# Probabilities turned as halves of 64 rows on two row groups, and new orders for four engines

## What is computed

```python
def dilated_mask(seq_len):           # SEGMENT_LENGTH = 64, DILATION_RATE = 4
    pos = jnp.arange(seq_len)
    seg = pos // SEGMENT_LENGTH
    local = seg[None, :] == seg[:, None]
    diff = jnp.abs(pos[None, :] - pos[:, None])
    dil = (diff > 0) & (diff % DILATION_RATE == 0) & (diff <= DILATION_RATE * SEGMENT_LENGTH)
    return jnp.where(local | dil, 0.0, -jnp.inf).astype(jnp.float32)
...
x = x + attention(_layernorm(x))     # 16 heads of 64, softmax over the allowed keys, then w_o
x = x + fp4_ffn(_layernorm(x))
x = x + gated_mixer(_layernorm(x))
x = x + token_mix(_layernorm(x))
```

## Time and profile before

| | us |
|---|---|
| median of 3 runs | 470.95 (470.03 to 474.9) |
| span of the profiled execution | 468.2 |
| TensorE busy | 443.3 |
| VectorE busy | 394.1 |
| ScalarE busy | 333.0 |
| GpSimd busy | 296.5 |

### The profile page before, as it was taken

How to read it: one execution, slowest core, us unless ns; L and a number is a source line. 1 busy time by engine, 2 the same in 40 slices (tenths; PEclk the granted TensorE clock), 3 DMA queues, 4 the chain that set the end, 5 groups by cost and what they waited for, 6 DMA issues and landing times.

```text
span 468.2 us, 17264 instructions
## 1 busy us (share of the span) xinstructions
PE 443.3 (95%) x6440; PEld 348.8 (74%) x6440; DVE 394.1 (84%) x1344; ACT 333.0 (71%) x975; POOL 296.5 (63%) x491
## 2 busy tenths in 40 slices
PE   7999699999999999999999899998987989999996
PEld 5687588888888888888787678887744757558775
DVE  5888598997988899799797697996899989998775
ACT  3678668778768777877786678695566579987533
POOL 4222576687576768667865587665669897674322
PEclk9999999999999999999999999999999999999999
DMA  6477952356345335445455564464000000000003
GB/s 224 175 254 201 276 122 53 75 115 123 75 84 110 74 74 109 81 78 109 86 116 122 110 135 90 77 123 91 1 1 0 0 2 0 2 0 2 1 0 91
DMA packets 136098, 40.53 MB, mean 87 GB/s; under 512 B 104976, under 2 KB 131024, under 8 KB 136016
## 3 DMA queue, kind: packets, MB, share of 16 engines
q1 hardware_dynamic: 135440, 38.38, 35.9%
q10 hardware_dynamic: 576, 1.05, 0.6%
HBM read 29.44 MB, written 9.96 MB: 84 GB/s over the span
## 4 chain that ended last, share of the span: by engine, by line
PE 59%; POOL 9%; DMA 8%; DVE 8%; ACT 7%; SPq 4%; issue 3%; ACTq 0%; POOLq 0%; DVEq 0%
PE psum L464 10%; PE psum L422 10%; PE psum L484 5%; PE psum L1186 5%; PE psum L498 5%; PE psum L495 4%; PE psum L510 4%; PE psum L403 4%; DMA st<-w_rows_dram 3%; DMA w_rows_dram<-st 3%; PE psum L1181 3%; ACT pband L569 3%; PE psum L405 2%; PE psum L404 2%; POOL area L1827 2%
## 5 line engine op out<-in xcount | busy, mean ns | idle before, releaser
L948 POOL TENSOR_SCALAR pband<-pband,fac 128x192 f32<-128x192 f32 x256 | 103.9, 424 | 84.8 <-DVE fac L771 84.7
L569 ACT ACTIVATE pband<-pband,st 128x192 f32<-128x192 f32 x256 | 113.2, 448 | 0.9 <-DVE st L719 0.9
L719 DVE CUSTOM_DVE_ANT_0 pband<-psum,band_mask 128x192 f32<-128x192 f32 x256 | 76.0, 353 | 0.1
L422 PE MATMUL psum<-keys,q_class 64*64 64x192 f32 (+2 forms) x1536 | 66.3, 274 | 0.0
L464 PEld LDWEIGHTS psum<-ident,pband 128*128 128x128 f32 x384 | 45.3, 141 | 25.5 <-issue 17.8
L464 PE MATMUL psum<-ident,pband 128*128 128x128 f32 x384 | 53.1, 273 | 6.1 <-DVE arena L836 3.1
L422 PEld LDWEIGHTS psum<-keys,q_class 64*64 64x64 f32 x1536 | 57.7, 133 | 1.4 <-issue 1.4
L569 ACT ACTIVATION_READ_ACCUMULATOR pband<-pband,st 128x1 f32 x256 | 49.5, 193 | 0.0
L938 POOL COPY q_class<-q_rows 128x512 f32<-128x512 f32 x32 | 36.4, 1137 | 14.0 <-ACT q_rows L609 14.0
L930 POOL COPY keys<-k_rows 128x512 f32<-128x512 f32 x32 | 36.2, 1131 | 14.3 <-issue 7.2
L780 DVE COPY pt<-psum 128x512 f32<-128x512 f32 x64 | 43.6, 682 | 0.4
(11 more groups left out here) (213 smaller groups left out, 1086.4 us busy)
## 6 DMA issues: line engine op xcount, KB each, us to landing
v_rows_dram<-arena SPq DMA_DIRECT2D x32, 256.0 KB, 4.6
v_both<-v_rows_dram SPq DMA_DIRECT2D x32, 256.0 KB, 3.9
v_seg<-v_rows_dram SPq DMA_DIRECT2D x64, 128.0 KB, 3.8
v_side<-v_rows_dram SPq DMA_DIRECT2D x96, 64.0 KB, 2.6
w_rows_dram<-st SPq DMA_DIRECT2D x64, 8.0 KB, 3.0
st<-w_rows_dram SPq DMA_DIRECT2D x64, 8.0 KB, 2.5
arena<-_attn_hidden_states_dram SPq DMA_DIRECT2D x4, 256.0 KB, 3.9
out_dram<-x SPq DMA_DIRECT2D x4, 256.0 KB, 2.5
```

The lines of the kernel that those rows point to most:

```text
L422: return pe.matmul(bank[2 * r + head][rows, at:at + y.shape[1]], x, y, start=True, stop=True, skip_group_check=True)
L569: act.activation(x, x, ACT.Exp, bias=mine[:, head:head + 1], scale=-1.0, accum_out=mine[:, 2 + head:3 + head]).then_inc(s_exp, 1)
L719: dve.tensor_tensor_reduce(pband[:, G % P_SLOTS, c, head, :], bank[2 * r + head][:, at:at + BAND], band_mask[:, (0, 1, 1, 2)[w], SEG * (1 ...
L948: pool.tensor_scalar(x, x, fac[:, F % 2, 1, c, head:head + 1], 1.0, ALU.mult, ALU.mult).then_inc(s_scaled, 1)
```

## The change

The four turns of a unit, four tiles of 128 by 128 each, become two, `turn(U, 0)` for the band's own part and `turn(U, 1)` for sides and segments. Each takes eight tiles, and each tile as two halves of 64 rows: the upper rows on the upper row group of the array into bank 4, the lower rows on the lower one into bank 5. A half is one transpose with 128 weight columns and 64 moving columns, so there are 32 of them for a unit where there were 16 of full height. VectorE copies bank 4 of both turns (`first_turned`), ScalarE bank 5 (`second_turned`): as many copies of the same size as before. `weigh` becomes `weigh_own`, `weigh_sides` and `weigh_segments` with the same products, and one semaphore `s_pv` counts them instead of two. `turn(U, 0)` waits for all eight scalings of the band. The order of the shared bank's tenants, the starts, the loops and the tails of TensorE, ScalarE, VectorE and GpSimd are laid out anew. SyncE's list stays, except for the counter that it waits on. The tables of `STEPS` change in their line breaks only.

```diff
-    occupants = [(0, "key")]
-    for x in range(1, FIRST_STEP):
-        occupants += [(x, "key"), (x - 1, "query")]
-    occupants.append((FIRST_STEP - 1, "query"))
-    for t in range(FIRST_STEP, NS_ALL + 8):
-        occupants += [(t - lag, who) for who, lag in (("key", 0), ("wo", 7), ("query", 0)) if there(t - lag)]
+    kinds = {"k": "key", "q": "query", "o": "wo"}
+    occupants = [(int(x[1:]), kinds[x[0]]) for x in (
+        "k0 k1 q0 k2 q1 k3 q2 k4 q3 k5 q4 q5 k6 q6 k7").split()]
+    for t in range(FIRST_STEP, DRAIN):
+        occupants += [(t - lag, who) for who, lag in (("wo", 6), ("query", -1), ("key", -2))
+                      if there(t - lag) and (t - lag, who) not in occupants]
+    occupants += [(x, who) for x, who in ((27, "wo"), (28, "wo"), (29, "wo"), (30, "wo"), (31, "wo"))]
...
-            def turn(U, b):
+            def turn(U, g):
                 if not there(U):
                     return
-                odd, e = b % 2, 2 * U + b // 2
-                if b < 3:
-                    pe.wait_ge(s_scaled, 8 * U + (4 if b == 0 else 8))
-                else:
+                pe.wait_ge(s_scaled, 8 * U + 8)
+                if g:
                     pe.wait_ge(s_segscaled, U + 1)
-                if U == 0 and b < 2:
-                    pe.wait_ge(s_vev[odd], V_TILES // 2)
-                wait(pe, s_pt[odd], e)
-                for k in range(4):
-                    if b < 2:
-                        src = pband[:, U % P_SLOTS, 2 * b + k // 2, k % 2, SEG * (k % 2):SEG * (k % 2) + P]
-                    elif b == 2:
+                for half in range(2):
+                    if U == 0 and g == 0:
+                        pe.wait_ge(s_vev[half], V_TILES // 2)
+                    wait(pe, s_pt[half], 2 * U + g)
+                for k in range(8):
+                    if g == 0:
+                        src = pband[:, U % P_SLOTS, k // 2, k % 2, SEG * (k % 2):SEG * (k % 2) + P]
+                    elif k < 4:
                         src = pband[:, U % P_SLOTS, k, :, :].rearrange("p h x -> p (h x)")[:, P:2 * P]
                     else:
-                        src = pseg[:, U % P_SLOTS, k, :, :].rearrange("p h x -> p (h x)")
-                    last = pe.transpose(turn_bank[odd][:, P * k:P * (k + 1)], src, ident[:, :])
-                last.then_inc(s_tr[odd], 1)
-
-            def weigh(U, b):
+                        src = pseg[:, U % P_SLOTS, k - 4, :, :].rearrange("p h x -> p (h x)")
+                    last = []
+                    for half in range(2):
+                        mine = slice(SEG * half, SEG * (half + 1))
+                        last.append(pe.transpose(turn_bank[half][:, SEG * k:SEG * (k + 1)], src[mine, :], ident[mine, mine]))
+                last[0].then_inc(s_tr[0], 1)
+                last[1].then_inc(s_tr[1], 1)
+
+            def turned(U, g):
+
+                return pt.rearrange("p (h s) x -> p h s x", h=2)[:, :, (2 * U + g) % PT_SLOTS, :]
+
+            def weigh_own(U):
                 if not there(U):
                     return
                 p, w = divmod(U, NW)
-                odd, e = b % 2, 2 * U + b // 2
-                if b == 0:
-                    wait(pe, s_out, U)
-                    pe.wait_ge(s_v[w], (p + 1) * V_DMAS[w])
-                if b == 2 and w < NW - 1:
+                wait(pe, s_out, U)
+                pe.wait_ge(s_v[w], (p + 1) * V_DMAS[w])
+                for half in range(2):
+                    pe.wait_ge(s_pt[half], 2 * U + 1)
+                by_class = out_bank.rearrange("q (h x c) -> q c h x", h=2, c=DIL)
+                for k in range(8):
+                    c, dims = k // 2, slice(DH * (k % 2), DH * (k % 2 + 1))
+                    last = pe.matmul(by_class[dims, c, :, :], v_both[:, c, w, dims], turned(U, 0)[:, :, SEG * k:SEG * (k + 1)],
+                                     start=k < 2, stop=False, skip_group_check=True)
+                last.then_inc(s_pv, 1)
+
+            def weigh_sides(U):
+                if not there(U):
+                    return
+                p, w = divmod(U, NW)
+                if w < NW - 1:
                     pe.wait_ge(s_v[w + 1], (p + 1) * V_DMAS[w + 1])
-                pe.wait_ge(s_pt[odd], e + 1)
-                turned = pt[:, PT_SLOTS * odd + e % PT_SLOTS, :]
                 by_class = out_bank.rearrange("q (x c) -> q c x", c=DIL)
+                for half in range(2):
+                    pe.wait_ge(s_pt[half], 2 * U + 2)
                 for k in range(4):
-                    if b < 2:
-                        c, head = 2 * b + k // 2, k % 2
-                        dims = slice(DH * head, DH * (head + 1))
-                        last = pe.matmul(by_class[dims, c, :], v_both[:, c, w, dims], turned[:, P * k:P * (k + 1)],
-                                         start=(b == 0 and k < 2), stop=False, skip_group_check=True)
-                        continue
                     for half in range(2):
-                        cols = slice(P * k + SEG * half, P * k + SEG * (half + 1))
                         side = 2 * w + 1 if half else 2 * w - 2
-                        if b == 2 and not 0 <= side < 2 * (NW - 1):
+                        if not 0 <= side < 2 * (NW - 1):
                             continue
                         for head in range(2):
                             dims = slice(DH * head, DH * (head + 1))
-                            if b == 2:
-                                last = pe.matmul(by_class[dims, k, SEG * half:SEG * (half + 1)], v_side[dims, k, side, :],
-                                                 turned[dims, cols], start=False, stop=False, skip_group_check=True)
-                            else:
-                                last = pe.matmul(out_bank[dims, cols], v_seg[dims, 2 * (TW * w + k) + half, :],
-                                                 turned[dims, cols], start=False, stop=(k == 3 and half == 1),
-                                                 skip_group_check=True)
-                last.then_inc(s_pv[odd], 1)
+                            pe.matmul(by_class[dims, k, SEG * half:SEG * (half + 1)], v_side[dims, k, side, :],
+                                      turned(U, 1)[dims, half, SEG * k:SEG * (k + 1)], start=False, stop=False,
+                                      skip_group_check=True)
+
+            def weigh_segments(U):
+                if not there(U):
+                    return
+                w = U % NW
+                for half in range(2):
+                    pe.wait_ge(s_pt[half], 2 * U + 2)
+                for k in range(4):
+                    for half in range(2):
+                        cols = slice(P * k + SEG * half, P * k + SEG * (half + 1))
+                        for head in range(2):
+                            dims = slice(DH * head, DH * (head + 1))
+                            last = pe.matmul(out_bank[dims, cols], v_seg[dims, 2 * (TW * w + k) + half, :],
+                                             turned(U, 1)[dims, half, SEG * (4 + k):SEG * (5 + k)], start=False,
+                                             stop=(k == 3 and half == 1), skip_group_check=True)
+                last.then_inc(s_pv, 1)
...
             for t in range(FIRST_STEP, DRAIN):
-                project(t, 1)
-                weigh(t - 6, 0)
-                weigh(t - 6, 1)
-                turn(t - 6, 3)
-                output(t - 7)
-                turn(t - 5, 0)
-                weigh(t - 6, 2)
-                scores(t - 2, 0)
-                weigh(t - 6, 3)
                 scores(t - 2, 1)
-                project(t, 0)
+                weigh_sides(t - 6)
+                weigh_segments(t - 6)
+                scores(t - 1, 0)
                 turn(t - 5, 1)
-                turn(t - 5, 2)
+                output(t - 6)
+                weigh_own(t - 5)
+                project(t + 1, 0)
+                turn(t - 4, 0)
+                project(t + 2, 1)
...
-                exp_difference(t - 4)
+                band_exps(t - 2, 0)
+                take_keys(t + 1)
+                seg_exps(t - 2)
                 take_out(t - 6)
-                take_queries(t)
-                odd_turned(t - 5, 1)
-                take_keys(t + 1)
-                band_exps(t - 2, 0)
-                odd_turned(t - 5, 3)
-                seg_exps(t - 2)
-                band_exps(t - 2, 1)
                 if t in (6, 7):
                     split_qk(1, 7 - t)
                 if t in (QUANT_STEP + 2, QUANT_STEP + 7, QUANT_STEP + 12):
                     coarse_weights((t - QUANT_STEP) // 5)
+                band_exps(t - 2, 1)
+                second_turned(t - 5, 1)
+                take_queries(t + 1)
+                second_turned(t - 4, 0)
+                exp_difference(t - 3)
...
-            def even_turned(U, b):
+            def first_turned(U, g):
                 if not there(U):
                     return
-                e = 2 * U + b // 2
+                e = 2 * U + g
```

(31 more changed lines are left out.)

210 lines of the change are left out of this document (107 added, 103 removed), and 16 rows, old and new, of the table STEPS.

## The result

The changed kernel takes 500.3 us (median of 4 runs, 497.1 to 504.4), the one before 471.8 beside it. Ratio 1.060, 95% interval 1.053 to 1.067. The forecast was 461.5 us and a range of 452 to 476. The profiled execution has a span of 498.6 us against 468.2: 30.4 us to find. Medians are over all runs of a kernel; in `e9`, `e10` and `e12` one run lies over 1.5% above the fastest, and the ratios leave it out.

The account below looks back on a forecast made before the run. TensorE's own issue rate was taken as the bound. Per step -0.86 + 0.30 + 0.21 = -0.35 us, over 24 intervals 8.4, plus 1 in the tail, takes the span from 468.2 to 458.8; time 461.5 us, range 452 to 476.

Parts of the forecast that it names:

- What bounds the kernel now: Whole loop: TensorE's own issue rate sets it, 9.26 us busy in a 9.26 us step.
- the part on the shared bank: Queries to keys: ScalarE's round trip through one bank takes 0.84 us, so TensorE waits 0.21 a step.
- Turns: TensorE's turns: 16 half pairs of 53 ns on two row groups replace 16 of 107, minus 0.86 us a step.
- The rival of row groups apart: Turns: halves do not run together, 478.7 us; chance 0.18 for over 470, shared with dearer shape changes.
- the rule on weight loads: Turns: a load overlaps matmuls only when the row group differs; otherwise a pair costs 107 ns, gain 0.
- Tile shapes and the shared bank: TensorE's step: three more shape changes cost 0.30 us, waiting for ScalarE's copy before keys 0.21.
- The leak at the keys: Before keys: only turn 0, 0.63 us with two changes, covers the 0.84 us round trip; TensorE waits 0.21.
- Evictions and the other engines: VectorE, ScalarE, GpSimd: instructions the same in number and size, only ordered anew; nothing priced.
- The start: 0, plus or minus 2: Kernel start: latency of loads and of the first exchange, so 0, plus or minus 2 us.
- the tail: 1 us gained: The four last windows, where TensorE waits in part: 1 us gained.
- The exchange stays hidden: Exchange of statistics: exp to use 10 to 11 us, scale to turn 2 to 3, spare about as before.
- VectorE becomes the bound: Loop: VectorE's waits return, quantise steps take 9.2 to 9.5 us, total 466 to 467; chance 0.20 for 465 to 470.

Follow-up runs that it names:

- e9: Kernel before, with VectorE's quantise parts moved right behind `factors(t - 4)`, which GpSimd's scalings start on; 470.8 us, ratio 0.995.
- e10: Changed kernel, with each engine's operations behind its last attention operation put into the relative order of the kernel before; 494.9 us, ratio 1.045.
- e12: Kernel before, with SyncE's own-value loads moved behind the fetch of statistics; 498.0 us, ratio 1.051.
- e17: Half turns in the orders of the kernel before, with `turn(t - 5, 0)` one group earlier, ahead of `project(t, 0)`; 486.1 us, ratio 1.037.
- e5: Changed kernel, with quantisation moved within VectorE's loop to where GpSimd waits for `factors`; 494.7 us, ratio 1.046.
- e6: Changed kernel, with VectorE's first normalisation and ScalarE's deviations ahead of the weight splits, as in the kernel before; 501.9 us, ratio 1.060.
- e16: Changed kernel without `weigh_sides(t - 6)` in TensorE's loop, attention output incomplete; 498.8 us in one run.
- e15: Changed kernel with the edits of e5, e10 and e6 and the value loads moved ahead in SyncE's queue; 473.6 us, ratio 1.011.
- e18: e15 with the side loads behind the statistics again for the last four units; 481.2 us, ratio 1.020.

## Why the prediction was wrong

*What bounds the kernel now* held: TensorE's issue set the loop before, all but the stretch from queries to keys, which the part on the shared bank rightly gives to ScalarE's round trip.

*Turns.* Minus 0.86 was forecast for pairs of 53 ns. The halves do run in pairs (30 to 37 ns a record), but a pair costs 60 to 75, and the groups fell by 0.48 us, some 0.1 of waiting for ScalarE's copy included. Right in sign, mis-sized by a third to almost a half. The rival of row groups apart, which the rule on weight loads would have given, is refuted: it needed over 88 ns.

*Tile shapes and the shared bank.* 0.30 and 0.21 were forecast; measured are 0.20 at the output and 0.11 at the queries. The leak at the keys is there as forecast, but too short for the list of waits: queries to keys are 1.64 us, as before and as forecast (1.6), because the keys start 0.05 us behind ScalarE's copy of the queries. The forecast took 0.63 us for the turn and 0.21 of waiting; the turn's slot is 0.74, with some 0.1 of waiting in it. Together -0.17 a step where -0.35 stood; steps of 9.10 and 8.63, not 8.9 and 8.45. This alone would have made about 466 us, an estimate. `e17` shows the leak where the cover is gone: 0.68 a step.

*Evictions and the other engines* is the step that failed: "the same in number and size, only ordered anew; nothing is priced". The same instructions take VectorE 25 us more. Moving them apart from GpSimd's made the kernel 5.6 us faster (`e5`) and, as part of the order behind the attention, the end 7.8 us shorter (`e10`).

*The start: 0, plus or minus 2* and *the tail: 1 us gained* failed with it. Their orders were rewritten, and I priced them as if only the turns had changed: +7.3 us at the start of the profiled pair (4.8 on average over kernels with either start, of which the repair of `e6` gives back 3.7), and +10.5 behind unit 25.

*The exchange stays hidden* held for the changed kernel (1.8 us of VectorE's waits for it in the loop), but "with about as much to spare" was luck: `e12` lost 24 us by one place in SyncE's list.

*VectorE becomes the bound*, the rival at 466 to 467, named the right engine by the wrong door. It looked at handshakes, not at instructions that grow. `e16` shows that taking work from TensorE no longer shortened the kernel.

Of the 12.6 us of the loop: minus 4 for the steps, plus 8 of stops, plus 3 of waits for `pt` and `pband` (4.6 against 1.6), some 2 of clock behind long stops; the other 3 to 4 are unplaced. The stops were in no rival. They are waits for instructions, as their places say; why the new orders meet them so much oftener is not settled.

## What to carry to other kernels

A new order of operations is a change to every one of them: price it by asking for each SBUF-only VectorE instruction which run of GpSimd's it comes in behind, and for each load what stands behind it in its queue. A gain of 2% on the busiest engine is only there while that engine is the bound; leave some of its work out once and see whether the time follows. The repaired start showed nothing alone (`e6`); with the other repairs the kernel took 473.6 us (`e15`) and, with the same loop, 481.2 (`e18`). An effect of 1% can't be read while 3 to 13 us of stops come and go, so compare the parts of the span, over several kernels that share the part.
